# An attention and expert kernel on one core: preparation and routing as units inside the attention's stages

## What is computed

```python
x = L0_attn_x                       # [B=4, T=1024, C=256]
xn = layernorm(x)
# attention: 16 heads of 64, causal
q, k, v = rope(xn @ Wq), rope(xn @ Wk), xn @ Wv
att = softmax(mask(q @ k.T / 8)) @ v @ Wo + bo
# experts: each of E=32 experts picks its K=8 tokens
probs = softmax(xn @ gate_w.T + gate_b, axis=tokens)     # per expert
vals, idx = top_k(probs, 8)
merged = sum over k of vals * xn[idx]                    # [B, E, C]
h = gelu([merged, 1] @ w1[e])                            # w1 [32, 257, 1024]
o = [h, 1] @ w2[e]                                       # w2 [32, 1025, 256]
ffn = scatter_add(idx, o * vals)
out = x + att + ffn
```

## Time and profile before

| | |
|---|---|
| median of 3 runs | 1484.44 us |
| the profiled execution's own time | 1488.41 us |
| its span, first to last instruction | 1486.6 us |
| TensorE busy | 1348.0 us (91%) |
| VectorE, ACT, GpSimd busy | 908.9, 623.9, 990.1 us |
| mean granted TensorE clock | 0.976 of 2.4 GHz |
| moved by DMA | 188.85 MB |

### The profile page before, as it was taken

How to read it: one execution, slowest core, us unless ns; L and a number is a source line. 1 busy time by engine, 2 the same in 40 slices (tenths; PEclk the granted TensorE clock), 3 DMA queues, 4 the chain that set the end, 5 groups by cost and what they waited for, 6 DMA issues and landing times.

```text
span 1486.6 us, 31037 instructions
## 1 busy us (share of the span) xinstructions
PE 1348.0 (91%) x11644; PEld 873.1 (59%) x11644; DVE 908.9 (61%) x1200; ACT 623.9 (42%) x919; POOL 990.1 (67%) x664
## 2 busy tenths in 40 slices
PE   3547988889898899999999999999999999999977
PEld 2424545545555467666666677666666776666646
DVE  7436656556565456666666765667666756666633
ACT  1214344424433433444544534444445444444541
POOL 1034556546555656788887866888878778888861
PEclk9779999999999899999999999999999999999999
DMA  5756757755776452212223222121232222212111
GB/s 201 273 196 219 250 174 237 252 181 190 261 265 210 142 161 79 76 62 76 75 88 108 84 76 76 58 72 66 80 115 80 90 81 68 76 59 73 45 48 57
DMA packets 112959, 188.85 MB, mean 127 GB/s; under 512 B 30064, under 2 KB 49936, under 8 KB 112432
## 3 DMA queue, kind: packets, MB, share of 16 engines
q1 hardware_dynamic: 85312, 115.39, 23.5%
q10 hardware_dynamic: 27456, 71.34, 14.2%
q0 software_dynamic: 48, 0.13, 0.0%
HBM read 130.58 MB, written 22.54 MB: 103 GB/s over the span
## 4 chain that ended last, share of the span: by engine, by line
PE 72%; DMA 9%; DVE 6%; issue 4%; ACT 2%; SPq 1%; POOL 0%; ACTq 0%; POOLq 0%
PE t_pO L1169 15%; PE t_pF L1144 11%; PE t_pA L1076 8%; PE t_pB L1076 6%; PE t_pF L1130 6%; DMA t_swap<-t_raw 6%; PE t_pC L1218 3%; PE t_pB L1218 3%; PE t_pA L1100 3%; PE t_pC L1100 3%; PE t_pA L1081 2%; PE t_pC L1178 2%; PE t_pB L1081 2%; DVE t_LO L964 1%; PE t_pC L1106 1%
## 5 line engine op out<-in xcount | busy, mean ns | idle before, releaser
L783 POOL TENSOR_TENSOR t_acc<-t_acc,t_PT 128x1024 f32<-128x1024 f32 (+3 forms) x256 | 435.9, 1703 | 146.5 <-ACT t_PT L818 126.7
L760 POOL TENSOR_TENSOR t_swap<-t_swap,s_sin 128x512 f32<-128x512 f32 x128 | 168.7, 1318 | 228.2 <-DMA t_swap<-t_raw 227.8
L1169 PE MATMUL t_pO<-t_PT,t_V 128*64 128x512 f32 (+3 forms) x1536 | 293.1, 503 | 4.4 <-ACT t_PT L818 4.4
L818 ACT ACTIVATE t_PT<-t_pA 128x1024 f32<-128x1024 f32 x192 | 169.7, 884 | 285.5 <-PE t_pA L1088 243.8
L1144 PE MATMUL t_pF<-t_xT,t_wqk 128*128 128x512 f32 x768 | 215.7, 417 | 19.9 <-DMA t_xT<-xt_s 11.9
L763 POOL TENSOR_TENSOR t_rot<-t_rot,t_swap 128x512 f32<-128x512 f32 x128 | 194.3, 1518 | 10.0
L964 DVE TENSOR_TENSOR t_LO<-t_rot,t_HI 128x512 fp32r<-128x512 f32 x128 | 150.1, 1172 | 82.2 <-ACT t_HI L849 82.0
L1169 PEld LDWEIGHTS t_pO<-t_PT,t_V 128*64 128x64 f32 x1536 | 93.7, 136 | 142.0 <-issue 118.7
L1144 PEld LDWEIGHTS t_pF<-t_xT,t_wqk 128*128 128x128 f32 x768 | 136.2, 190 | 62.4 <-issue 29.4
L940 DVE TENSOR_REDUCE s_nm<-t_pC 128x2 f32<-128x256 f32 (+2 forms) x96 | 71.7, 775 | 146.6 <-PE t_pC L1106 146.6
L839 ACT ACTIVATE t_raw<-t_pF 128x512 f32<-128x512 f32 x128 | 76.4, 597 | 194.8 <-PE t_pF L1144 143.7
(11 more groups left out here) (153 smaller groups left out, 2464.7 us busy)
## 6 DMA issues: line engine op xcount, KB each, us to landing
t_w1t<-in_L_ffn_w ACTq DMA_DIRECT2D x32, 1024.0 KB, 6.6
t_swap<-t_raw SPq DMA_DIRECT2D x256, 128.0 KB, 2.1
t_w2t<-in_L_ffn_w ACTq DMA_DIRECT2D x32, 1024.0 KB, 9.5
t_OT<-r_s SPq DMA_DIRECT2D x128, 128.0 KB, 3.0
t_wqk<-wqk_s SPq DMA_DIRECT2D x24, 512.0 KB, 4.2
xt_s<-a_xThl SPq DMA_DIRECT2D x16, 512.0 KB, 3.5
t_xT<-xt_s SPq DMA_DIRECT2D x8, 1024.0 KB, 8.2
t_wvs<-wv_s SPq DMA_DIRECT2D x12, 512.0 KB, 3.6
```

Source lines behind the costliest of these rows:

```text
L760: pool.tensor_tensor(swap[:, r % 2, :], swap[:, r % 2, :], sin[:, c * BANK:(c + 1) * BANK], ALU.mult).then_inc(sin_done, 1)
L783: pool.tensor_tensor(a[:, :, off:], a[:, :, off:], pt, ALU.add).then_inc(acc_done, 1)
L818: act.activation(PT[:, n % PTS, :, 0:w], bank[:, :, 0:w], ACT.Exp, scale=SCALE).then_inc(exp_done, 1)
L1169: mm = pe.matmul(pO[h * DH:(h + 1) * DH, off:], v, PT[:, n % PTS, h, 0:w], start=(j == 0), stop=(j == 4 * c + 3))
```

## The change

One block is left; `prepare_block` and `route_block` are gone.

- **Batch 0 alone is prepared ahead.** x of batch 0 comes in two halves. ACT normalises the first four tiles, GpSimd the other four. Sixteen transposes go into `pA` and `pB`, and high and rest are written straight into `xT`: batch 0 does not pass through DRAM. The first stage also waits for the masks (`halves_loaded`), the rotary tables and the constants.
- **Batches 1 to 3** are normalised by ACT (`NORM_AT`) from the last stage of period -2 to stage 4 of period -1; VectorE takes their statistics in stages (-2, 5) and (-1, 0), and batch 1's ahead of the loop. Transposes, logits, the gates' transposes, the merge and the transposed merge are 24 "units" (`UNITS_AT`) from (-1, 0) to (2, 0), through the second banks of `pC` and `pB`; TensorE waits in the following stage for their readers (`unit_read`). The top eight are chosen at (1, 2), the weights made at (1, 3).
- **The experts** start three periods later (`MOE = 3`): first layers from period 2, group G in period G + 3, the last in period 10.
- **Batch 0's heads** are stored to DRAM (`o0_s`) half by half as they are normalised, since the units' tiles lie in `OT` and batch 1 writes `OT` before the output is due. Batch 0's outputs run in periods 11 and 12, one tile a stage from (11, 2) to (12, 3); for each, SyncE loads `os` (0.5 MB in pieces of 512 bytes), ACT rounds it at the end of the stage before.
- **Wo** is loaded raw and split at (11, 0) (ACT, then VectorE), and not stored. ACT waits there for the load.

```diff
+MOE = 3
+STAT = 10
...
-    if P == -1:
+    G = P - MOE
+    if G == -1:
...
+    if MOE + E // GE <= P <= MOE + E // GE + 1:
+        n = (P - MOE - E // GE) * GROUPS + g - 2
+        return [(0, n)] if 0 <= n < NT else []
...
+UNITS_AT = {(-1, 0): [("x", 1, 0, 0)], (-1, 1): [("x", 1, 0, 1)], (-1, 2): [("logit", 0, 0), ("x", 1, 1, 0)],
+            (-1, 3): [("logit", 0, 1), ("x", 1, 1, 1)], (-1, 4): [("logit", 1, 0), ("x", 2, 0, 0)],
+            (-1, 5): [("logit", 1, 1), ("x", 2, 0, 1)], (0, 0): [("x", 2, 1, 0)], (0, 1): [("x", 2, 1, 1)],
+            (0, 2): [("logit", 2, 0), ("x", 3, 0, 0)], (0, 3): [("logit", 2, 1), ("x", 3, 0, 1)],
+            (0, 4): [("x", 3, 1, 0)], (0, 5): [("x", 3, 1, 1)], (1, 0): [("logit", 3, 0)], (1, 1): [("logit", 3, 1)],
+            (1, 4): [("gates", 0), ("gates", 1)], (1, 5): [("merge",)], (2, 0): [("merged",)]}
+SQRT_AT = {(-2, 4): 1, (-2, 5): 2, (-1, 0): 3}
+NORM_AT = {(-2, 5): [(1, 0), (1, 1)], (-1, 1): [(2, 0)], (-1, 2): [(2, 1)], (-1, 3): [(3, 0)], (-1, 4): [(3, 1)]}
...
+                n = normalise_of(*STAGES[s - 4]) if s >= 4 else None
+                if n is not None and n < 2 * PAIRS:
+                    sp.wait_ge(o_done, n + 1)
+                    sp.dma_start(o0_s[n // 2, :, n % 2 * BANK:(n % 2 + 1) * BANK],
+                                 OT[:, n // 2, n % 2 * BANK:(n % 2 + 1) * BANK]).then_inc(o0_stored, 16)
...
+                for y, t in next_outputs(s):
+                    if y == 0:
+                        if t:
+                            sp.wait_ge(ol_done, t)
+                        sp.wait_ge(o0_stored, 2 * PAIRS * 16)
+                        sp.dma_start(os[:, :, :], o0_s[:, :, t * P128:(t + 1) * P128].rearrange("p r t -> r p t")).then_inc(os_loaded, 16)
...
+                if y == 0:
+                    act.wait_ge(os_loaded, (t + 1) * 16)
+                    act.wait_ge(wo_lo, 1)
...
+                if (P, g) == (MOE - 1, 0):
+                    act.wait_ge(unit_done, UNIT["merge",] + 1)
+                    load_w1(0)
+                    load_w1(1)
...
+                if (P, g) == (MOE + E // GE, 0):
+                    act.wait_ge(wo_loaded, 16)
+                    act.activation(woh[:, 0, :, :], woraw[:, :, :], ACT.Copy).then_inc(wo_hi, 1)
...
+                    b, c, k = u[1:]
+                    i = 2 * (b - 1) + c
+                    dve.wait_ge(xs_hi, 2 * i + k + 1)
+                    dve.tensor_tensor(xs[:, i % 2, 1, k, :], bank, xs[:, i % 2, 0, k, :].bitcast(F32), ALU.subtract).then_inc(unit_read, 1)
...
+            dve.wait_ge(g_trans, 1)
+            dve.wait_ge(g_zero, 1)
...
+            statistics(0)
+            moments(0)
+            statistics(1)
+            for c in range(2):
+                for k in range(KT):
+                    i = 2 * c + k
+                    dve.wait_ge(x0_hi, i + 1)
+                    dve.tensor_tensor(xT[:, c, 1, k, :], (pA, pB)[c][:, k, :], xT[:, c, 0, k, :].bitcast(F32), ALU.subtract).then_inc(x0_lo, 1)
...
+            pe.wait_ge(g_copied, B)
+            pe.wait_ge(x0_lo, 2 * KT)
+            pe.wait_ge(halves_loaded, 8 * 16)
+            pe.wait_ge(const_made, 6)
...
+                    pe.wait_ge(unit_read, units_before(s))
                     scores(P, *chunks[1])
...
+                for u in units:
+                    if u[0] != "merge":
+                        unit(u)
```

More of the change, by code:

```diff
@@ L596, in next_outputs, with unit_bank, units_before @@
             return outputs_of(*STAGES[s + 1]) if s + 1 < len(STAGES) else []
+        def unit_bank(n):
+            return (pC, pB)[n % 2][:, 1, :]
+        def units_before(s):
+            return sum(len(UNITS_AT.get(t, ())) for t in STAGES[:s])
         def slot_bank(n):
@@ L728, in _ @@
                     if g == 0:
+                        for u in range(2):
+                            sp.wait_ge(xs_stored[u], (B - 1) * 16)
                         sp.wait_ge(proj_done, FILL["q", P + 1, 0] + 1)
@@ new lines, in _ @@
+            act.dma_start(gw[:, :], gate_w).then_inc(g_loaded, 16)
+            for b in range(B):
+                act.dma_start(gb[b * E:(b + 1) * E, :], gate_b.rearrange("(e a) -> e a", a=1)).then_inc(gb_loaded, 16)
+            act.wait_ge(g_copied, B)
+            act.activation(gThl[:, 0, :, :, :], gT[:, :, :, :], ACT.Copy).then_inc(g_hi, 1)
+            root(0)
+            normalise(0, 0)
+            for c in range(2):
+                for k in range(KT):
+                    i = 2 * c + k
+                    act.wait_ge(x0_done, i + 1)
+                    act.activation(xT[:, c, 0, k, :], (pA, pB)[c][:, k, :], ACT.Copy).then_inc(x0_hi, 1)
@@ L1017, in output, with statistics @@
                 dve.tensor_tensor(yt[:, t % 2, :], out_bank(t), xb[:, t % 2, :], ALU.add).then_inc(y_done, 1)
-            dve.wait_ge(zeroed, 3)
-            merged(0)
+            def statistics(b):
+                for t in range(NT):
+                    if b == 0 and t % 4 == 0:
+                        dve.wait_ge(x0_loaded[t // 4], 16)
+                    elif t == 0:
+                        dve.wait_ge(xb_loaded[b - 1], 16)
+                    st = dve.bn_stats(stats[:, b, t, :], xn[:, b, t, :])
+                st.then_inc(stat_done, 1)
@@ L1213, in output @@
                 pe.wait_ge(ol_done, n + 1)
-                pe.wait_ge(wo_loaded, 16)
+                pe.wait_ge(wo_lo, 1)
                 a = 0
@@ L1251, in _ @@
                     turn_maxima(P + 1, 0)
-                if banks and (slots or outputs_of(P, g) or normalise_of(P, g) is not None):
+                if banks and (units or slots or outputs_of(P, g) or normalise_of(P, g) is not None):
                     pe.wait_ge(max_done, MAXES[P, g] + 1)
+                for u in units:
+                    if u[0] != "merge":
+                        unit(u)
                 for x_ in slots:
@@ L1258, in _ @@
                     output(y, t)
+                for u in units:
+                    if u[0] == "merge":
+                        unit(u)
                 for x_ in slots:
```

704 lines of the change are left out of this document (346 added, 358 removed).

## The result

The changed kernel took 1497.58 us (median of 7 runs, 1487.27 to 1501.37), the kernel before 1481.77 us beside it (7 runs, 1477.22 to 1486.54): ratio 1.0094, 95% interval 1.0063 to 1.0126. I had forecast 1470.6, 27.0 us less, and a gain.

A forecast was written before the change was run, and what follows sets the result against it. Chains in which TensorE waits bound the front; behind the experts, TensorE's instructions cost full time. Terms 86.5 + 137 + 443.6 + 805.7 = 1472.8 us, 13.8 below the span 1486.6; carried to the median, 1470.6, range 1447 to 1492.

The forecast's parts named there:

- Term 1: Time until the first fill: from 89.1 us to 22, between 18 and 30.
- second way: Before the first fill, the masks' DMAs queue on SyncE behind 5.25 MB, 23 us; high end 30 if masks come last.
- Term 2: Run-in to the first scores: from 33.6 us to 50, as stages grow by 16; between 42 and 62.
- clock rival: In the longer, thinner run-in TensorE's clock stays down, giving 1485 us, no change; 14.5 us over forecast, chance 0.12.
- Term 3: First two stages with scores: from 17.9 us to 14.5, between 12 and 18.
- term 4: Periods 0 to 2, with gates, merge and group 0's first layers: from 152.2 us to 137, between 124 and 150.
- Term 5: Periods 3 to 10 and batch 0's outputs: 408 + 27.6 + 8 = 443.6 us, between 430 and 467.
- The stores: Eleven 0.25 MB stores ahead of swaps in the expert periods, 1.1 us each: 3 us taken, between 0 and 12.
- `os` rival: In batch 0's outputs ACT's wait for `os` costs 26 us instead of 8, taking the gain; chance 0.17.
- carrying over to the median: Whole run: the spans' difference, 13.8 us, subtracted from the median 1484.4, giving 1470.6 us.
- 54 us that were expected in front: Gain ahead of period 0's copy, which was to move from 140.6 us to 86.5.

The follow-up runs named there:

- e2: Changed kernel with ACT reading each stage's units before normalising a later batch's tiles in period -1: 1491.5 us, ratio 1.0083 to the kernel before.
- e3: Changed kernel with TensorE waiting for the reader of the unit before the last, not of the last: 1492.5 us, ratio 1.0064 to the kernel before.
- e12: Changed kernel without statistics and small operations of batches 2 and 3, batch 1's used instead (output wrong): 1485.9 us, ratio 1.0020 to the kernel before.
- e8: e4 plus eight unread filler matmuls at the end of each stage of period -1: 1487.7 us, ratio 1.0040 to the kernel before.
- e1: The changed kernel again, unchanged, for a second profile: 1497.0 us, ratio 1.0101 to the kernel before.
- e10: e5 with each finished half of batch 0's heads stored twice: 1482.7 us; without one far-off run, ratio 1.0009 to the kernel before.
- e11: e5 with experts and batch 0's outputs one period later still (`MOE = 4`): 1469.1 us, ratio 0.9919 to the kernel before.
- e5: e4 with the load of `os` issued ahead of the swap and its wait for `raw`: 1470.8 us, ratio 0.9925 to the kernel before.
- e6: e4 with Wo split at (11, 1) instead of (11, 0), a stage after its load is issued: 1481.4 us, ratio 1.0009 to the kernel before.
- e9: The kernel before the change, unchanged, profiled a second time: one execution, 1482.7 us, span 1481.0.
- e4: Changed kernel with the edits of both e2 and e3: 1480.7 us, ratio 1.0007 to the kernel before.
- e13: e5 with the store of each half of batch 0's heads issued behind the stage's swap: 1472.1 us, ratio 0.9917 to the kernel before.

## Why the prediction was wrong

- **Term 1** (22 us) was right to 0.2 us, though by its second way: the chain ends with the masks' DMA, as the high end had it, and the data path was ready at 21.1 (the weights' rest). The two ways are within 1 us of each other here.
- **Term 2 is the step that failed.** "Four stages so grow by about 3 us, and two by 1.8 us behind ACT's eight normalised tiles in a row": 50 us were 67 to 68, outside its own high end of 62. I had priced what each unit adds and left the rest of the stage as it was. What the runs show in its place is that a stage is the sum over one chain through four engines: ACT's tiles in stages (-1, 1) to (-1, 4) stood ahead of the unit's copies (e2: 5.2 us), TensorE waited for the reader of a unit that uses the other bank (e3: 3.3), and the two batches' statistics were 6.3 of their 10.7 us on the chain (e12). These removals add up to 14.8 us where 17 were missing, and so the chain is shown to be the pace of the run-in. They are no partition of the 17, though: e3 also took out waits that I had priced, the eight tiles' 4.0 us in stage (-2, 5) are on the chain and in none of them, and the clock has a share (next point). The tiles' 0.51 us instead of 0.385 is inside the first. A list of VectorE's work, 36.9 us, was right (35.4 busy) and told nothing, since no engine was full.
- **The clock rival** had the sign right and the place, 0.75 instead of 0.85 in the run-in, and has a share of the miss that the terms did not carry. The fills of the last four stages of the run-in took 6.6 us together in the kernel before (in both profiles) and 11.0 and 10.7 in the changed one, and in the first profile they stand on the chain: some 4 us of the 17, against the 14.5 that the rival gave. The filler did not win it back (e8). By the rule of the Trainium skill that I cited ("TensorE: Matmul & The Clock Gate", "HAM oscillation — how this bites in real kernels"), gaps send the clock down and the work behind them starts slow; the trace agrees there: from 40 to 50 us the granted clock was 0.50, TensorE idled twice for VectorE, 4.1 and 2.3 us, and the fill at 54.2 us took 2.87. It does not tell every slow fill: those at 22.0 and 26.4 us took 2.9 us each in a stretch whose recorded clock is 1.00.
- **Term 3** (14.5, was 12.1) and **term 4** (137, was 134 to 136) held, merge and choice included.
- **Term 5** was 6.7 us short in periods 3 to 10 by e1. The stores, "nothing if none is on the path, 12 us if all are; I take 3", seem to be at the upper end: a second set cost 11 us by the medians and 12.8 by the profiles (e10). If so, something pays for the first set, since the first seven expert intervals took 363.0 in e1 and 363.2 before; that the later periods split no weights is the candidate, but e11, a period later still, won 1.6 with an interval that covers zero, so it was not shown. The excess stands in interval 10: 51.8 in e1, where the last expert interval before, less two output tiles, was 51.4 - 6.9 = 44.5. There `start_output` holds up a swap (6.69 us in e1's chain) and ACT waits for Wo and for `os`; e5 got 1.7 us of it back, e6 0.3. With the wait for Wo gone, e6's chain still has that swap, 6.81 us long, and no run moved the loads ahead of it: the rest is open.
- **The `os` rival** had the mechanism right and was not what decided: periods 11 and 12 cost 35.5 us over two steady ones where I had 35.6. That the sum hit is luck in part: with the load ahead of the swap (e5) they cost 95.3 - 69.2 = 26.1 us, less than the 27.6 that I had for the matmuls alone. So a tile costs less than 3.45 us, and waiting cost over 9 us where I had 8.
- **The carrying over to the median** missed 7.7 us of the 27.0: the profile that I started from was 4.0 us above its median, e1's is 3.7 below the changed kernel's. Then 19.3 are left, and the terms give 17.0 for the run-in, - 2.4 for the two stages behind it, - 1.5, + 6.7, and - 0.6 for the others: 19.2.

Of the 54 us that were expected in front, 37 to 39 came (period 0's copy at 101.3 us in e1 against 138.4 in e9 and 140.6 in the profile that I started from); a run-in twice as long took the rest. What came was given back in the periods behind, where the experts and batch 0's outputs now stand, with stores that the kernel before did not have. e5, three edits of order and waits away, has 1470.8 us, 0.75% faster than the kernel before; e11, 1469.1, is not distinguishable from it.

## What to carry to other kernels

When work is dissolved into the stages of a run-in that no engine fills, don't add up engines: write one stage as a chain, in the order in which each engine's queue has it, and ask of every instruction that is put in whether it stands ahead of something that another engine waits for. Put work without a deadline behind the reads of the stage, wait for the bank and not for the last user, and issue a load ahead of the wait for the swap if ACT waits for it. Before a gain of 1% is forecast, look at how far the profiled execution lies from its median: here that was over a quarter of the miss.

## What I had not expected of the hardware

- Executions of one kernel vary more than the effect of an edit: e4's ten runs fall in two groups, six from 1478.2 to 1480.7 and four from 1485.7 to 1488.9.
- Four tiles of 128x256 on ACT with scale and bias per partition took 2.06 us, 0.51 each, against 0.385 for a copy of that size from PSUM; a single tile's record was 0.588 us long. No run tells the operands from the source.
- By two profiles a further store of 0.25 MB on SyncE's queue cost the kernel 1.2 us beside the experts' loads, and nothing without them (e10), while the swaps' median did not rise. One queue position instead of the other made no difference that five runs could see (e13).
